# Attention on one Trainium2 core: the key-side causal mask moved into the score operands and onto GpSimd

## What is computed

```
scores = einsum('bhqd,bhkd->bhqk', q, k) * scale      # 2048 x 2048 per head
scores = scores + alibi_bias                          # second attention only; -inf above the diagonal
attn   = softmax(scores, axis=-1)
ctx    = einsum('bhqk,bhkd->bhqd', attn, v)
```

## Time and profile before

| | |
|---|---|
| median of 3 runs | 2074.77 us (2068.17 to 2075.59) |
| the profiled execution | 2063.22 us |
| its span | 2061.1 us |
| TensorE busy | 1801.9 us (87%) |
| VectorE busy | 1600.7 us (78%) |
| ScalarE busy | 1112.6 us (54%) |
| GpSimd busy | 545.0 us (26%) |

### The profile page before, as it was taken

The page is one execution under the profiler, slowest core; times in us unless marked ns, Lnnn a source line. Parts: engine busy times, 40 slices in busy tenths (PEclk is TensorE's granted clock), DMA queues, the critical chain, the costliest instruction groups (busy, mean ns, idle before and its releaser), DMA issues. The chain is left out here.

```text
span 2061.1 us, 46755 instructions
## 1 busy us (share of the span) xinstructions
PE 1801.9 (87%) x18108; PEld 914.8 (44%) x18108; DVE 1600.7 (78%) x3423; ACT 1112.6 (54%) x2075; POOL 545.0 (26%) x568
## 2 busy tenths in 40 slices
PE   6777788999799999998899977777778999999967
PEld 2222254444255555554544422222543555555454
DVE  5899966666788999993565559999668999999545
ACT  5543423222278888885322264444353888888815
POOL 2798931000200000000100028989330000000022
PEclk9899999999789999998799989999886999999969
DMA  5333400311302333211031104443012233322100
GB/s 176 113 127 111 133 12 0 83 46 36 109 25 50 54 53 56 53 28 22 2 86 48 31 13 128 128 117 118 1 53 69 48 58 57 59 58 42 30 5 21
DMA packets 68266, 126.80 MB, mean 62 GB/s; under 512 B 20919, under 2 KB 30676, under 8 KB 66572
## 3 DMA queue, kind: packets, MB, share of 16 engines
q1 hardware_dynamic: 67628, 123.27, 23.5%
q10 hardware_dynamic: 416, 0.54, 0.1%
HBM read 105.15 MB, written 16.84 MB: 59 GB/s over the span
## 5 line engine op out<-in xcount | busy, mean ns | idle before, releaser
L1648 ACT ACTIVATE a_probs<-a_ps_k 128x512 f32<-128x512 f32 (+3 forms) x1280 | 598.3, 545 | 221.9 <-PE a_ps_k L1562 126.4
L1544 PE MATMUL a_ps_q<-a_k_op,a_q_op 84*32 84x512 bf16 (+7 forms) x5120 | 536.6, 366 | 22.7 <-DVE a_maxes L1705 9.5
L1708 DVE TENSOR_REDUCE a_maxes<-a_ps_q 128x1 f32<-128x512 f32 x768 | 504.1, 685 | 66.8 <-PE a_ps_q L1544 63.9
L1558 PE MATMUL a_ps_k<-a_q_op,a_k_op 87*32 87x512 bf16 (+7 forms) x5120 | 519.2, 353 | 2.4 <-ACT a_probs L1648 0.6
L1580 PE MATMUL a_ps_o<-a_probs,a_vh 128*32 128x512 f32 (+3 forms) x2752 | 319.8, 508 | 0.8 <-ACT a_probs L1648 0.8
L1544 PEld LDWEIGHTS a_ps_q<-a_k_op,a_q_op 72*32 72x32 bf16 (+1 forms) x5120 | 187.5, 97 | 170.1 <-DVE a_maxes L1708 69.9
L1705 DVE CUSTOM_DVE_ANT_0 a_ps_q<-a_ps_q,all_c_mask_q 128x128 f32<-128x128 f32 (+3 forms) x512 | 248.0, 495 | 2.6 <-PE a_ps_q L1544 1.3
L1558 PEld LDWEIGHTS a_ps_k<-a_q_op,a_k_op 75*32 75x32 bf16 (+1 forms) x5120 | 186.1, 96 | 134.3 <-ACT a_probs L1648 82.6
L979 ACT ACTIVATE e_silu<-e_psg,all_me_b 128x512 f32<-128x512 f32 x128 | 87.8, 687 | 227.5 <-PE e_psg L911 227.4
L1788 POOL CAST a_max_parts<-a_neg_max 128x16 bf16<-128x16 f32 x32 | 6.3, 198 | 747.8 <-DVE a_neg_max L1713 747.8
L1062 DVE SCALAR_TENSOR_TENSOR e_mid<-e_psv,all_me_b,e_silu 128x512 f32<-128x512 f32 x128 | 95.7, 749 | 129.8 <-PE e_psv L913 125.9
(11 more groups left out here) (263 smaller groups left out, 2393.1 us busy)
## 6 DMA issues: line engine op xcount, KB each, us to landing
m0sc_c_rows<-m_bc_rows SPq DMA_DIRECT2D x32, 512.0 KB, 3.5
e_w_rows<-e_comb SPq DMA_DIRECT2D x64, 256.0 KB, 3.2
m1sc_c_rows<-m_bc_rows SPq DMA_DIRECT2D x32, 512.0 KB, 3.6
a_q_op<-a_q_parts SPq DMA_DIRECT2D x30, 288.0 KB
a_k_op<-a_k_parts SPq DMA_DIRECT2D x30, 288.0 KB
a_outputs<-a_o_sb SPq DMA_DIRECT2D x480, 18.0 KB
m0sc_b_rows<-m_bc_rows SPq DMA_DIRECT2D x32, 256.0 KB
m1sc_b_rows<-m_bc_rows SPq DMA_DIRECT2D x32, 256.0 KB
```

The source lines that it names most:

```text
L1544: last = pe.matmul(ps_q[32 * r:32 * r + 32, use % QB, 0:width], q_op[h % SLOT][0:NR, part(t, r)], k_op[h % SLOT][0:NR, kc * CH:kc * CH + w ...
L1558: last = pe.matmul(ps_k[32 * r:32 * r + 32, b % KB, 0:width], k_op[h % SLOT][:, part(j, r)], q_op[h % SLOT][:, c * CH + first:c * CH + fir ...
L1648: act.activation(probs[:, n % PSLOT, 0:width], ps_k[:, b % KB, 0:width], ACT.Exp).then_inc(exp_done, 1)
L1708: dve.tensor_reduce(found, bank, AX.X, ALU.max).then_inc(q_read, 1)
```

## The change

1. **Scores.** The four mask matmuls of each diagonal item go. The operands get three more rows (`STEP`, `NR_STEP` = 78 and 90): on the query side -1e30 or 0, on the key side 0 or 1, which together put -1e30 on those whole groups of 32 columns in which every key of a 32-row group is later than the query. A diagonal item is now two stretches: its first 128 columns with the longer operands, the rest with the shorter ones. The item of width 128 has the first stretch alone.
2. **Probabilities.** What lies above the diagonal in the diagonal 32 x 32 squares is set to zero after the exponential, by one `affine_select` on GpSimd of 128 x 128 elements for each diagonal item (16 a head), in place in `probs`. `times_v` waits for them on a new semaphore `cleared`.
3. **Order.** `times_v` of four items is issued one item later, after the scores and the query item that follow.
4. **GpSimd's queue.** The selections stand in it by chunk; `place(h + 2)` comes before those of chunk 1, `split_maxima(h + 1)` before those of chunk 3. In the last head the sums `upper` of chunks 0 and 1 come before the selections of chunk 3.
5. **Loads.** Four more small DMAs at the start (the step rows of the queries); the rows of ones become six rows; the constant `mask_k` is no longer loaded.

```diff
-                d = j - TPC * c
-                for r in range(4):
-                    last = pe.matmul(ps_k[32 * r:32 * r + 32, b % KB, 0:width], k_op[h % SLOT][:, part(j, r)],
-                                     q_op[h % SLOT][:, c * CH + first:c * CH + first + width], start=True, stop=d < 0,
-                                     skip_group_check=True)
-                for r in range(4 if d >= 0 else 0):
-                    last = pe.matmul(ps_k[32 * r:32 * r + 32, b % KB, 0:P], g["ident_b"][:, part(0, r)],
-                                     g["mask_k"][:, :], start=False, stop=True, skip_group_check=True)
+                stretches = [(NR_MAX, 0, width)]
+                if j >= TPC * c:
+                    stretches = [(NR_STEP, 0, P), (NR_MAX, P, width)]
+                for rows, lo, hi in stretches:
+                    for r in range(4 if lo < hi else 0):
+                        last = pe.matmul(ps_k[32 * r:32 * r + 32, b % KB, lo:hi], k_op[h % SLOT][0:rows, part(j, r)],
+                                         q_op[h % SLOT][0:rows, c * CH + first + lo:c * CH + first + hi],
+                                         start=True, stop=True, skip_group_check=True)
                 last.then_inc(k_ready, 1)
...
                 pe.wait_ge(exp_done, NK * h + n + 4)
+                if n + 3 in ends:
+                    pe.wait_ge(cleared, TPC * (NC * h + c + 1))
...
                         stream(turn, item, NQ + LEAD + b, NQ + LEAD + b + 1)
-                    times_v(h, n)
+                        if a == n and b:
+                            times_v(*divmod(b - 4, NK))
+                    if h == LAST and n == NK - 4:
+                        times_v(h, n)
...
+            def clear_later_keys(h, c):
+
+                for n in range(ends[c] - TPC + 1, ends[c] + 1):
+                    pool.wait_ge(exp_done, NK * h + n + 1)
+                    pool.affine_select(out=probs[:, n % PSLOT, 0:P], in_=probs[:, n % PSLOT, 0:P], pattern=[[1, P]],
+                                       compare_op=ALU.is_ge, fill=0.0, base=0, channel_multiplier=-1).then_inc(cleared, 1)
...
             place(0)
+            split_maxima(0)
+            place(1)
             for h in range(HEADS):
-                split_maxima(h)
-                if h + 1 < HEADS:
-                    place(h + 1)
-            pool.wait_ge(k_ready, NK * LAST)
-            pool.wait_ge(o_back, 16 * BACKS * LAST)
+                for c in range(NC):
+                    if c == 1 and h + 2 < HEADS:
+                        place(h + 2)
+                    if c == NC - 1 and h + 1 < HEADS:
+                        split_maxima(h + 1)
+                    if c == NC - 1 and h == LAST:
+                        pool.wait_ge(o_back, 16 * BACKS * LAST)
+                        add_upper(0)
+                        add_upper(1)
+                    clear_later_keys(h, c)
...
             for s in range(SLOT):
-                sp.dma_start(k_op[s][NR:NR_MAX, :], dram["ones_b"]).then_inc(ones_loaded, 16)
+                sp.dma_start(k_op[s][NR:NR_STEP, :], dram["ones_steps"]).then_inc(ones_loaded, 16)
+                sp.dma_start(q_op[s][NR_MAX:NR_STEP, :], dram["steps"]).then_inc(ones_loaded, 16)
```

More of the change, by code:

```diff
@@ L50 @@
 ALIBI = 12
+STEP = 3
 NEG = -1e30
@@ L1351, in attention @@
         NR_MAX = NR + SPL
+        NR_STEP = NR_MAX + STEP
         SLOT = 4
@@ L1381, in attention @@
             inv = ml.sb("inv", [P, JT])
-        q_op = [m.sb(f"q_op{s}", [NR_MAX, TOK], BF16) for s in range(SLOT)]
-        k_op = [m.sb(f"k_op{s}", [NR_MAX, TOK], BF16) for s in range(SLOT)]
+        q_op = [m.sb(f"q_op{s}", [NR_STEP, TOK], BF16) for s in range(SLOT)]
+        k_op = [m.sb(f"k_op{s}", [NR_STEP, TOK], BF16) for s in range(SLOT)]
         vh = [m.sb(f"vh{s}", [P, NT, 32]) for s in range(SLOT)]
@@ L1429, in attention @@
         pv_done = m.sem("pv_done")
+        cleared = m.sem("cleared")
         o_read = m.sem("o_read")
@@ L1606, in _ @@
             stream(turn, item, 0, NQ + LEAD)
-            pe.wait_ge(ones_loaded, 16 * SLOT)
+            pe.wait_ge(ones_loaded, 2 * 16 * SLOT)
             pe.wait_ge(v_copied, NC)
@@ L1793, in split_maxima, with add_upper @@
                 pool.tensor_tensor(part(2), max_rest[:, :], part(1), ALU.subtract).then_inc(max_ready, 1)
+            def clear_later_keys(h, c):
[3 more added lines that the diff above has]
+                                       compare_op=ALU.is_ge, fill=0.0, base=0, channel_multiplier=-1).then_inc(cleared, 1)
+            def add_upper(c):
+                pool.wait_ge(last_back[c], 16 * 4)
+                if c >= 2:
+                    pool.wait_ge(total_ready, c - 1)
+                pool.tensor_tensor(upper[:, c % 2, :], oT[:, 2, chunk(c)], oT[:, 3, chunk(c)], ALU.add).then_inc(upper_ready, 1)
             for r in range(rounds):
@@ L1811, in _ @@
             place(0)
+            split_maxima(0)
+            place(1)
             for h in range(HEADS):
[L1813 to L1817 removed]
+                for c in range(NC):
[8 more added lines that the diff above has]
+                    clear_later_keys(h, c)
             for c in range(NC):
[L1819 removed]
                 if c >= 2:
[L1821 to L1822 removed]
+                    add_upper(c)
                 ahead.power(pool, c)
@@ L1996, in constants @@
             sel_head[h, b, b, h] = 1
+    later = np.arange(TOK)[None, :] % P // 32 >= np.arange(1, STEP + 1)[:, None]
     slopes = (2.0 ** (-8.0 / HEADS * (np.arange(HEADS, dtype=np.float32) + 1.0))).astype(np.float32)
@@ L2017, in constants @@
         "c_mask_q": np.where(np.arange(CH)[None, :] - (CH - P) > k, NEG, 0.0).astype(np.float32),
-        "c_mask_k": np.where(k > q, NEG, 0.0).astype(bf),
         "c_sel_head": sel_head.reshape(P, SB, P),
@@ L2021, in constants @@
         "alibi_k": ka.astype(bf),
-        "ones_b": np.ones((SPL, TOK), np.float32).astype(bf),
+        "ones_steps": np.concatenate([np.ones((SPL, TOK), np.float32), later.astype(np.float32)]).astype(bf),
+        "steps": np.where(later, 0.0, NEG).astype(bf),
     }
```

2 lines of the change are left out of this document (1 added, 1 removed).

## The result

The changed kernel takes 2104.18 us (median of 4 runs, 2103.73 to 2105.76) beside 2072.15 us for the kernel before in the same session (4 runs, 2068.17 to 2075.59): a ratio of 1.0159, with a 95% interval of 1.0138 to 1.0180. It is slower by about 32 us, where 2056 us and a gain were forecast; the time lies outside the range of 2040 to 2085 us as well. The profiled execution took 2103.73 us.

The account below looks back on a forecast made before the run. TensorE and VectorE were taken to wait for each other in turn through three `ps_q` banks. 0.80 less 0.10 us a head over 29 heads, less 1.3 at the ends, gave 2074.8 - 19 = 2056 us; range 2040 to 2085.

Parts of the forecast that it names:

- the one on the value products: ScalarE's copy of a finished chunk waits for the later product about 0.5 us four times a head, costed at nothing.
- the later product upsets ScalarE: Rival: each chunk's copy lets TensorE wait 0.3 us, 1.2 us a head, 2091 us; chance 0.06.
- The later products as a gain: Value products one item later, in TensorE's order: between -0.1 and +0.34 us a head, raising 0.63 to 0.80 taken.
- The masks: Dropping 64 mask matmuls a head on TensorE gains 0.63 us a head.
- the three stretches: Parts of a head where TensorE leads until VectorE waits for a bank; forecast gains 0.20, 0.216 and 0.216 us.
- The selections: GpSimd's selections take 0.4 us each, range 0.29 to 1.03; up to 0.65 us each they are free.
- The dear selection: Rival: from 0.65 us each, value products wait for GpSimd; about 2225 us at 1.03 us each; chance 0.16.
- Their side effect on VectorE: GpSimd's selections hold up VectorE's masked reductions by up to 0.15 us where they meet; 0.1 us a head lost.
- The number of heads: The gain counts while query items stream: 14.6 heads in each attention, 29 in all.
- The ends: At the end of each attention the product falls behind waits for the spreads: +0.65 us, twice 1.3.
- The power of the next layer norm: At an attention's end, GpSimd's 1.03 us power waits for the last selections; costed at nothing.
- The sum 20.3 - 1.3: Gain of 0.70 us a head over 29 heads, 20.3 us, less 1.3 us at the attentions' ends: 19 us.

Follow-up runs that it names:

- e3: The changed kernel with ScalarE copying a finished chunk out one exponential later, products still late: 2074.8 us, ratio 1.0019, 24.55 us a head.
- e2: The kernel before with only the value products issued one item later, masks by matmul and no selections: 2114.8 us, ratio 1.0207, 25.95 us a head.
- e14: e3 with the 512-wide exponentials over 448 columns only: 2078.51 us, ratio 1.0031, 24.45 us a head.
- e6: e3 with the query items one item less ahead (LEAD 13 in place of 14): 2080.84 us, ratio 1.0045, 24.58 us a head.
- e1: The changed kernel with the value products back at the end of their own four items: 2061.14 us, ratio 0.9955, 24.09 us a head.
- e5: The changed kernel with the products back in place and without selections or the wait for them: 2061.35 us, ratio 0.9970, 24.08 us a head.
- e12: e1 with VectorE's plain reductions over 448 of 512 columns: 2045.62 us, ratio 0.9889, 23.57 us a head.
- e10: e1 with the 512-wide exponentials over 448 columns only: 2066.7 us, ratio 0.9982, 24.09 us a head.
- e4: The changed kernel, products late, without selections or the products' wait for them: 2100.34 us, ratio 1.0141, 25.54 us a head.
- e13: e8 with the next layer norm's first power issued before the last selection in the last head: 2059.44 us, ratio 0.9957, 24.08 us a head.
- e8: e1 with the query items one item further ahead (LEAD 15 in place of 14): 2059.47 us, ratio 0.9947, 24.07 us a head.

## Why the prediction was wrong

**The step that failed** is the one on the value products: "ScalarE now waits for the product before it copies a chunk out, about 0.5 us four times a head; ... the scores of the fourth item behind need its next exponential 1.3 us after the product, and copy and exponential take some 1.1 us. I cost that at nothing". The mechanism was seen, the cover named, and both of its numbers were off. The rows above give 1.33 us for the path (0.19 from the product's end to the copy, 0.50 for the copy, 0.64 for the exponential and its signal) and 1.04 us for the cover, since the query items issued there are narrow. Two estimates with a margin of 0.2 us between them were booked as a certainty. The price that I gave without the cover, "up to 0.3 us four times a head", was about right: 0.29 us in the row shown, 1.03 us a head by e3. It stood as the rival "the later product upsets ScalarE", 2091 us, at a chance of 0.06.

**The later products as a gain** (0.91 by stretches, 0.80 taken, in place of 0.63 us a head): wrong in sign. In e2 the shift costs 1.55 us a head, in the changed kernel 1.49; even without the copy's wait (e3) it costs 0.46 and gives nothing. Of these 0.46 us at least 0.10 are ScalarE's by e14, and none are the lead's by e6. What makes up the rest stays open. VectorE's waits for filled banks over 640 to 880 us come to 15.0 us in e3 and 13.8 us in e1, but there are 52 in place of 30, so a part may lie in the three banks between TensorE and VectorE; no run separates that from ScalarE.

**The masks: 0.32 us a head** (24.40 less 24.08 in e5, 24.09 in e1) in place of 0.63. The first of the three stretches gave nearly what was said: VectorE's idle time at its end, 0.11 us, is gone and the stretch is 0.16 us shorter, where 0.20 were forecast. The other two gave 0.08 us each, not 0.216. TensorE in e1, and then VectorE, show why:

```profile
729.04 0.39 PE L1547 MATMUL a_ps_q<-a_k_op,a_q_op 72*32 72x512 bf16 x4
...
729.76 0.39 PE L1547 MATMUL a_ps_q<-a_k_op,a_q_op 72*32 72x512 bf16 x4
729.98 0.29 PE L1564 MATMUL a_ps_k<-a_q_op,a_k_op 78*32 78x128 bf16 x8
730.23 0.40 PE L1547 MATMUL a_ps_q<-a_k_op,a_q_op 72*32 72x512 bf16 x4
```

```profile
729.48 0.69 DVE L1713 TENSOR_REDUCE a_maxes<-a_ps_q 128x1 f32<-128x512 f32 x1 [0.40 <-PE a_ps_q L1547]
```

The eight matmuls at 729.98 have 256 columns in all, 0.11 us of TensorE by the rate of the earlier trace rows; the next query item comes after 0.25 us. It needs the bank that the query item of 729.04 filled. VectorE, having waited for it, reduces it from 729.48 to 730.17, and at 730.23 the bank is written again: a round trip of 1.19 us, in which TensorE now has only 1.05 us to do. I had looked for VectorE's next wait, where the stretch that TensorE leads ends, and not for the bank's round trip inside it. e12 confirms it: with a reduction shorter by 0.067 us these two stretches, from VectorE's timeline, shrink from 2.336 to 2.269 us and from 2.283 to 2.214, by 0.067 and 0.069 us, one reduction each. Had TensorE alone led there, they would have stayed as they were. ScalarE (e10) and GpSimd (e5) have no share in it. The split of the scores itself cost what was reckoned, 0.06 us a quartet of 128 columns.

**The selections:** 0.292 us each, at the low end of 0.29 to 1.03, where I took 0.4; no value product waits for one in the steady part, as forecast. The dear selection (0.16) did not come. The Trainium skill's count of about 12 cycles an element for loops that branch (GPSIMD Engine Reference, "Elementwise - side-by-side cycle accounting") would have made it 1.3 us, by the estimate in the prediction; the row shows 0.292 us, the price of a copy, so the selection does not go by that count.

**Their side effect on VectorE,** 0.1 us a head: not found. e1 and e5 differ by 0.01 us, the changed kernel and e4 by 0.04. I had held the trace against the rule of the Trainium skill (SBUF - State Buffer, "SBUF: two separate sides") that such reductions, with one input in PSUM, are not locked out; within 0.04 us a head the runs agree with the rule. What held up the one masked reduction beside GpSimd's split of the maxima was not tried. In the changed kernel it is again 0.47 us long beside the same split, but the next one starts 0.38 us after it and not 0.48, so 0.10 of the 0.15 us that I read as a hold-up by GpSimd have another cause.

**The number of heads** (29) held: 29 by 1.18 are 34.2 us, the two attentions took 35.5 more. **The ends** of +0.65 us each: 0.68 us in the place that I priced; to the last sum +1.6 us in the first attention and -0.5 in the second, which is within the scatter of such ends. The power of the next layer norm, booked at nothing, did make the normalise wait: 1.15 us in the changed kernel and 1.09 in e1; by e13 at most some 0.3 us of that counted. **The start** cost nothing, as forecast. The sum 20.3 - 1.3 was therefore right in its count and wrong in its factor: +0.70 us a head forecast as a gain, -1.18 measured. With the measured terms it reads 0.32 for the masks and selections less 1.49 for the late products, of which 1.03 are the copy.

**The chances.** 0.20 for slower was too little: a margin of 0.2 us between two estimates on a path that repeats 128 times deserved a chance near one half.

Of the kernels that leave nothing out, e8 and e13 are the fastest, 0.5% and 0.4% below the one before: the new masks without the later products. They differ from e1 by no more than the intervals.

## What to carry to other kernels

When a producer is issued later, write down, for every engine that waits for it, what stands behind that wait in the same queue, and follow it to the first instruction that another engine needs. If path and cover are within 0.3 us of each other, take the durations row by row at that very place, and don't book the result at nothing. A copy that nobody needs soon belongs behind the work that others wait for: moving it by one exponential gave back 1.03 of 1.49 us a head.

Work taken from an engine that waits for another in turn through a few banks is gained only down to the banks' round trip (here fill, reduction and two signals, 1.19 us). To find out what holds a loop, shorten one suspect by a known amount and see how far the period follows: reductions shorter by 0.067 us gave 0.52 us a head, exponentials shorter by 0.053 us gave nothing. Where they do give something, the amount tells that the suspect has a share and not how large it is.

## What the runs showed of the hardware

- An `affine_select` of 128 x 128 elements in f32 takes 0.292 us on GpSimd (512 of them; the four of a chunk lie within 1.19 us), the same as a copy of that size (0.29).
- 16 of them a head beside VectorE's 40 reductions cost at most 0.04 us of 25.6.
- Eight small DMAs in a row are issued 0.31 to 0.34 us apart, each 0.26 to 0.29 us of the queue.
- An exponential takes 0.597 us for 128 x 512 elements and 0.544 us for 128 x 448 on ScalarE; a row maximum takes 0.69 and 0.62 us on VectorE.
